# Attention rounds that prepare the first pair of head groups of the round after them, with half of the slot transfers begun from the scalar engine's own DMA queue

## What is computed

```python
x = window_attention(x)       # 16 heads of 16, window 64, rotary
x = gated_ffn(x)              # sigmoid(x Wr) * (relu(x Wk)^2 Wv), with a shift by one token
x = linear_attention(x)       # elu + 1 features, no softmax
h = layernorm(x); x = x + causal_attention(h) @ Wproj   # 16 heads, softmax over up to 1024 keys
x = x + moe(layernorm(x))     # 8 experts, top 2, capacity 1024
```

## Time and profile before

| | us |
|---|---|
| three runs, median (lowest, highest) | 2194.8 (2194.42, 2198.81) |
| the profiled execution | 2197.95 |
| its span in the trace | 2196.2 |

### The profile page before, as it was taken

How to read it: one execution, slowest core, us unless ns; L and a number is a source line. 1 busy time by engine, 2 the same in 40 slices (tenths; PEclk the granted TensorE clock), 3 DMA queues, 4 the chain that set the end, 5 groups by cost and what they waited for, 6 DMA issues and landing times. The chain is left out here.

```text
span 2196.2 us, 33587 instructions
## 1 busy us (share of the span) xinstructions
PE 1874.8 (85%) x11092; PEld 1115.5 (51%) x11092; DVE 1030.1 (47%) x2379; ACT 900.9 (41%) x1855; POOL 684.8 (31%) x991
## 2 busy tenths in 40 slices
PE   4998699899889989996998999699844999999990
PEld 2566345555443655554355555433332666666660
DVE  2456465487375547745744784576430000000014
ACT  1453255446527443662554465347511222222212
POOL 4203234213253320326232132532144233333220
PEclk8999799999979999997999999889956999999995
DMA  5600305520141543005044400423032233333215
GB/s 162 83 2 1 91 7 76 74 29 1 41 96 29 64 64 41 2 21 112 26 59 60 59 1 1 92 56 48 2 105 89 70 75 77 77 68 65 43 17 163
DMA packets 96381, 123.47 MB, mean 56 GB/s; under 512 B 15328, under 2 KB 69536, under 8 KB 96048
## 3 DMA queue, kind: packets, MB, share of 16 engines
q1 hardware_dynamic: 81360, 104.39, 23.8%
q0 software_dynamic: 14848, 16.85, 4.7%
HBM read 44.85 MB, written 25.58 MB: 32 GB/s over the span
## 5 line engine op out<-in xcount | busy, mean ns | idle before, releaser
L948 ACT ACTIVATE b_probs<-b_psum 128x512 f32<-128x512 f32 (+3 forms) x896 | 430.6, 538 | 266.2 <-PE b_psum L821 255.9
L1187 DVE TENSOR_REDUCE b_mneg<-b_psum 128x2 f32<-128x384 f32 (+5 forms) x608 | 337.8, 593 | 150.3 <-PE b_psum L805 144.8
L805 PE MATMUL b_psum<-b_qk 96*128 96x192 bf16 (+4 forms) x1280 | 325.9, 325 | 10.9 <-DVE b_mhalf L1187 5.6
L821 PE MATMUL b_psum<-b_qk 99*128 99x512 bf16 (+5 forms) x1344 | 295.0, 295 | 12.1 <-ACT b_probs L948 6.7
L836 PE MATMUL b_psum<-b_probs,b_v 128*32 128x512 f32 (+5 forms) x2688 | 234.3, 424 | 1.4 <-issue 1.3
L1552 DVE TENSOR_TENSOR b_ye<-b_psum,b_b2b 128x512 f32<-128x512 f32 x32 | 22.1, 692 | 429.1 <-PE b_psum L1507 423.6
L1507 PE MATMUL b_psum<-b_w,b_hid 128*128 128x256 f32 x1024 | 222.4, 379 | 0.8 <-ACT b_hid L1531 0.8
L1498 PE MATMUL b_psum<-b_xgt,b_w 128*128 128x512 f32 x512 | 222.2, 594 | 0.0
L1531 ACT ACTIVATE b_hid<-b_psum,b_b 128x512 f32<-128x512 f32 x128 | 88.0, 688 | 318.3 <-PE b_psum L1498 317.6
L1507 PEld LDWEIGHTS b_psum<-b_w,b_hid 128*128 128x128 f32 x1024 | 193.9, 190 | 27.6 <-ACT b_hid L1531 1.6
L821 PEld LDWEIGHTS b_psum<-b_qk 99*128 99x128 bf16 x1344 | 125.2, 100 | 145.4 <-ACT b_probs L948 72.7
(11 more groups left out here) (212 smaller groups left out, 2611.5 us busy)
## 6 DMA issues: line engine op xcount, KB each, us to landing
b_qk<-b_split SPq DMA_DIRECT2D x324, 128.0 KB, 5.8
b_w<-in_W SPq DMA_DIRECT2D x16, 1024.0 KB
b_qk<-b_split SPq DMA_DIRECT2D x120, 64.0 KB, 2.6
b_src<-in_x SPq DMA_DIRECT2D x4, 1024.0 KB, 5.7
before_last_norm<-b_early SPq DMA_DIRECT2D x4, 1024.0 KB, 4.5
b_o<-before_last_norm SPq DMA_DIRECT2D x4, 1024.0 KB
before_last_norm<-b_o SPq DMA_DIRECT2D x4, 1024.0 KB
normed<-b_y SPq DMA_DIRECT2D x4, 1024.0 KB, 4.5
```

What stands on the lines that cost most here:

```text
L805: ins = pe.matmul(out[:, i, :], q[0:KS, h, P * t:P * t + P], q[0:KS, HG + h, a:e], start=not last, stop=True, skip_group_check=True)
L821: ins = pe.matmul(out[:, i, :], q[0:KM, HG + h, P * t:P * t + P], q[0:KM, h, a:e], start=not windowed[g], stop=True, skip_group_check=True)
L948: act.activation(probs_of((g, h2, t))[:, heads[0]:heads[-1] + 1, a - BANK * h2:e - BANK * h2], bank, ACT.Exp, scale=SCALE).then_inc(s.exp_ ...
L1187: dve.tensor_reduce(out, in_bank(("max",) + x[1:], heads, e - a), AX.X, ALU.max, negate=True).then_inc(s.max_read, 1)
```

## The change

The rounds become: 4 near groups; then three rounds of 4 near and 4 far groups; then 4 far groups; then the route alone. The device loop is gone, the rounds are written out. Each of the three middle rounds also prepares the pair that the next round begins with (`coming`): a near pair of the next batch in the first two, for which `source`, `fetch` and `refill` are done again late in the round (behind `h_turn` and `out1`), and a far pair in the third. A round whose first pair is ready omits it and begins with its maxima. The second round isn't ready: it loads its own input (`own_x`) and prepares its pair 0 itself. Buffers of `qk` are given by a table. Group 8 takes the buffer of group 6, and group 9 that of group 4. At its end a round waits until the loads of the coming pair have landed. The 6 transfers of each group into the k half are a new kind, `send`, begun by ACT on its own queue. Group 0 is copied in halves only where the round isn't ready. Beside that `k1_exp` writes into `u.o` instead of a buffer of its own, and `v1_sum` comes after `k_feat`.

```diff
+QK_OF = {4: (0, 1, 2, 1, 0, 1), 8: (0, 1, 2, 0, 1, 2, 0, 2, 0, 1), 0: ()}
...
-    LANDING = {"load": 9.0, "spread": 2.2, "source": 3.0, "x3_in": 3.0, "x3_out": 3.0, "x4_out": 3.0, "z_out": 3.0}
+    LANDING = {"load": 7.0, "send": 7.0, "spread": 2.2, "source": 3.0, "x3_in": 3.0, "x3_out": 3.0, "x4_out": 3.0, "z_out": 3.0}
...
+        def fetch(late):
+            add(("source", late), "SP", 6.0, ("h_turn", 1, NC - 1) if late else None)
             for y in range(2):
                 for c in range(NC):
-                    add(("fetch", y, c), "PE", 0.45, ("source",))
-                    add(("refill", y, c), "ACT", 0.6, ("fetch", y, c))
+                    add(("fetch", late, y, c), "PE", 0.45, ("source", late), ("out1", 3) if late else None)
+                    add(("refill", late, y, c), "ACT", 0.6, ("fetch", late, y, c))
...
-            last = ("power",) + self.last_piece(g - RING, 1) if g >= RING else None
+            last = ("power",) + self.last_piece(self.behind(g), 1) if self.behind(g) is not None else None
...
-                        add(("load", g, a, slot, y), "SP", 0.46 if y is not None else 0.64, (kind, g // 2, q), last)
+                        add((("load", "send")[a], g, a, slot, y), ("SP", "ACT")[a], 0.46 if y is not None else 0.64, (kind, g // 2, q), last)
...
-        prep(0)
+        pairs = groups // 2 + (coming is not None)
+        if self.fetched:
+            fetch(0)
+        if not first:
+            prep(0)
         prep(1)
...
-            if n in (2, 4) and n + 2 < groups:
+            if n and n % 2 == 0 and n // 2 + 1 < pairs:
+                if n // 2 + 1 == groups // 2 and coming:
+                    fetch(1)
                 prep(n // 2 + 1)
...
+                if coming is not None:
+                    load_done(sp, groups + n)
...
+                elif kind == "send":
+                    send_slot(act, x)
...
-            attend(near, 0, later=later)
-            attend(far + near + far, 1)
-            with nc.Fori(1, B - 1) as b:
-                attend(far + near + far, b + 1, b - 1)
-            attend(far + far, None, B - 2)
-            attend((), None, B - 1)
+            attend(near, ahead=0, later=later)
+            for b in range(1, B):
+                more = b < B - 1
+                attend(near + far, ready=b > 1, ahead=b, own_x=rows_of(b) if b == 1 else None, coming=more,
+                       coming_x=rows_of(b + 1) if more else None, route=b - 2 if b > 1 else None)
+            attend(far, ready=True, route=B - 2)
+            attend((), route=B - 1)
```

More of the change, by code:

```diff
@@ L240, in place_of, with behind @@
     def place_of(self, g):
-        return self.of_kind[self.windowed[g]].index(g)
+        return self.of_kind[self.windowed[g]].index(g) if g < self.groups else g - self.groups
+    def behind(self, g):
+        return max((x for x in range(g) if self.qk_of[x] == self.qk_of[g]), default=None)
     def count_shared(self):
@@ L564, in load_done @@
     def load_done(eng, g, y=None):
-        if g:
-            eng.wait_ge(loaded[g], 16 * 2 * SLOTS)
-        else:
-            for n in range(2) if y is None else (y,):
-                eng.wait_ge(loaded[groups + n], 16 * 2 * SLOTS)
+        if g >= 2 or not ready:
+            if g:
+                eng.wait_ge(loaded[g], 16 * 2 * SLOTS)
+            else:
+                for n in range(2) if y is None else (y,):
+                    eng.wait_ge(loaded[2 * NG + 2 + n], 16 * 2 * SLOTS)
     def done(eng, *x):
@@ L617, in attend_and_pass_on, with send_slot @@
     sem = s._asdict()
+    def send_slot(eng, x):
+        _, g, a, slot, y = x
+        part = [slot in slots for slots in SLOTS_OF[a]].index(True)
+        eng.wait_ge((s.high_done, s.mid_done, s.low_done)[part], 4 * (g // 2 - plan.first) + (4 if y is None else 2 * y + 2))
+        if plan.behind(g) is not None:
+            eng.wait_ge(s.exp_done, order[("power",) + plan.last_piece(plan.behind(g), 1)] + 1)
+        cols = slice(0, T) if y is None else slice(BANK * y, BANK * y + BANK)
+        eng.dma_start(u.qk[plan.qk_of[g]][HD * slot:HD * slot + HD, HG * a:HG * a + HG, cols],
+                     u.split[HG * HD * (g % 2):HG * HD * (g % 2 + 1), a, part, cols]
+                     ).then_inc(loaded[g if g else 2 * NG + 2 + y], 16)
     xa = u.xa[:, :, 1:T + 1]
@@ L767, in _ @@
                     first = 2 * (plan.place_of(2 * g) // 2)
-                    if near and next_x is not None and t == 0 and not first:
-                        pe.wait_ge(s.fetched, 4)
+                    if t == 0 and 2 * g == groups and not near:
+                        done(pe, "h_take", 1, NC - 1)
+                    elif t == 0 and near and (2 * g == groups or own_x is not None):
+                        pe.wait_ge(s.fetched, 2 * NC * (1 + (2 * g == groups and own_x is not None)))
                     x_rows = u.xa[:, :, 1:T + 1] if near else u.xt
@@ L777, in _ @@
                 elif kind == "fetch":
-                    pe.wait_ge(s.src_in, 16)
-                    _, y, c = x
+                    _, late, y, c = x
+                    pe.wait_ge(s.src_in, 16 * (2 if late and own_x is not None else 1))
                     for t in range(4):
@@ L921, in _ @@
                         done(act, "k1_sum", k)
-                        if k >= 2:
-                            done(act, "k_feat", k - 2)
-                        act.wait_ge(s.added, NT * (groups // 2))
-                        ins = act.activation(u.kexp[k % 2], u.kfeat[:, half(k)], ACT.Exp, bias=u.minus[:, :])
+                        ins = act.activation(pair(u.o, k), u.kfeat[:, half(k)], ACT.Exp, bias=u.minus[:, :])
                     elif kind == "q_exp":
```

91 lines of the change are left out of this document (47 added, 44 removed).

## The result

The changed kernel takes 2297.4 us against 2196.8: ratio 1.046, 95% interval 1.042 to 1.050, so 100.6 us slower. I had said 2190, at most 2216.

The account below looks back on a forecast made before the run. PE, busy for 85% of 2196.2 us, was taken as the bound. Terms of 0 - 5 + 0 + 4 - 4 = -5 us against the profiled 2197.95 gave 2192.95; that execution lies 3.15 above the median, so 2190 us, range 2146 to 2216.

Parts of the forecast that it names:

- Boundaries, 0 each: At the three boundaries between rounds, PE's loss would be 32.1 us each against 32.0 before, so 0 each.
- my mark of 25 to 35: The prediction counts as wrong if the loss at a boundary between rounds leaves the span of 25 to 35 us.
- The rival that two queues overlap: At round ends, 24 transfers take 15 us on two queues; with other gains -44 us, 2151 in all; chance 0.25.
- PE's useful time stays, and only the lost time can change: At boundaries, work is moved, not removed: middle rounds still prepare four pairs each, so only PE's lost time can change.
- My own mark against me: The prediction counts as wrong if the stretches between boundaries lose over 10 us more or less.
- The first round, -5 (0 to -9): At the first round's start, two issuers begin the 64 KB transfers sooner: -5 us, bounds 0 and -9.
- The second round, 0 (-6 to +8): At the second round's start, waiting for its own input is paid back by shorter first maxima: 0, between -6 and +8.
- Maxima, -4 (-17 to +5): Inside rounds, maxima transfers have less ahead of them with half the slot transfers in the other ring: -4 us, -17 to +5.
- ACT's issues, +4 (0 to +35): In far stretches, issues moved to ACT stand between exponentials PE waits for, most of them hidden: +4 us, 0 to +35.
- Near stretches get worse: Rival: near groups come first and wait for their second pair's transfers, six more us in three rounds: 2207; chance 0.10.

Follow-up runs that it names:

- change_same_order_one_queue: The changed kernel with every compute engine's order kept and the scalar engine's 204 transfers merged into the sync engine's queue, against the kernel before: ratio 1.048.
- all_on_sync: The changed kernel with the k halves of a slot begun by the sync engine again, so one queue for all transfers, against the kernel before: ratio 1.036.
- before_landing_seven: The kernel before with only the planner's time from a slot's issue to its use lowered from 9 to 7 us: ratio 0.989, 2167.1 us.

## Why the prediction was wrong

**Boundaries, 0 each: right in size.** Predicted was 32.1 us each, measured is 93.2 / 3 = 31.1, though the third, at 35.4, lies just outside my mark of 25 to 35. By the finer count they won 4 us each. PE's idle time there was 18.5 to 21.1 us (said: about 20), the first exponentials came at 13.5 us (said: 12), and 24 transfers took about 25 us (bound 1.04 us each; I took 0.95). The rival that two queues overlap is out: 128 and 136 GB/s, where I had asked for 180. The rule in the Trainium skill, "DMA: Bandwidth & Descriptors", section "Issuing engines are not separate DMA queues", would have put the sum 7 us higher. Here the trace and change_same_order_one_queue agree with it: same order, one queue or two, 1.048 and 1.046. It has no price for a second issuer, though, and there is one: in the kernel before the same comparison is 1.018 and 1.031.

**The step that failed: "PE's useful time stays, and only the lost time can change", counted at the boundaries alone.** I took the bodies over at the loss they had in the kernel before, but for two small terms. My own mark against me was 10 us in the bodies. They lose 20 to 23 us more each. The boundaries did trade evenly. What changed is what had been taken as given, PE's waits inside the rounds, above all for transfers:

- **The buffer table** stood in the diff and in the words on the change, and the sum had no term for it. It costs 1.0 to 1.4%, 22 to 31 us. A slot transfer that becomes possible one group later is moved just when PE needs the maxima.
- **The first round, -5 (0 to -9): measured +24.** 15 of these are the table. Another 5 are the second round's input: PE waits 11.9 us behind the barrier where it waited 6.6. Its first exponentials came at 69.87, as in the earlier trace rows. The two queues didn't shorten the start; all_on_sync, with one, has them at 66.64. SP's own 18 issues at the start took from 38.23 to 55.21, 17 us for half of the 36 that had taken 24.92.
- **The second round, 0 (-6 to +8): measured about +44,** or about +32 without its new end, which belongs to the boundaries. A ready round saves a head, but the second isn't ready. It has a near head that waits for its input and its own slots: the head lost 36.1 us where 21.9 were lost, and its body 51.6 where 29.0 were. With the table and the urgency mended it is 406.6 us, against 367.5 in before_landing_seven. Of these 39 us, 13 are the moved pair and 12 the wait for b_mrow near its end. The remaining 14 aren't parted by any run. The head's wait, and the longest one of the body, in the changed kernel:

```profile
257.22 0.48 PE L814 MATMUL b_psum<-b_id,b_src 128*128 128x128 f32 x1 [11.93 <-DMA b_src<-in_x]
```
```profile
343.23 0.27 PE L851 MATMUL b_psum<-b_mask_k,b_id 128*128 128x128 bf16 x1 [8.19 <-DMA b_qk<-b_mrow]
```

- **Maxima, -4 (-17 to +5): measured +36.9** in PE's waits. What stands ahead of the maxima is set by when slots become possible and by the plan more than by how many queues there are: at the same order these waits are 81.4 us with one queue and 71.8 with two.
- **ACT's issues, +4 (0 to +35): +1.0%, 22 us,** inside the bounds, but partly by luck. The same order with all issues on SP is no faster. The 22 us are the order that the planner makes once ACT has 204 steps more; I costed an issue by its 0.64 us and never a new plan. The mechanism that I priced is there as well, 18 us more of PE's waiting for ACT at the same order, but two queues save at least as much in waiting for transfers.
- **LANDING** had no term either; it was worth -1%.

**Near stretches get worse**, with chance 0.10 and 6 us a round, was the rival that came nearest. It named the right wait (slots and maxima behind the second pair's transfers), but has a part of the loss only: near groups' waits for b_mrow in the three middle rounds are 41.7 us, where they were 30.5. PE's waits of 8.2 us at 343, 7.4 at 730, 6.8 at 815, 5.4 at 1135 and 7.2 at 1221 are all for near groups. The far groups, which had none before, have 22.6 us, among them 4.8 at 1359 and 7.4 at 1615. The range ended at 2216, since each rival was summed alone and none had the bodies, the first round and the second worse together.

How the 4.6% are made up, as far as the runs part it: the planner's number -1.1%; the table 1.0% (one queue); the late end of the round 2.4% by leaving the transfers out, of which 0.7% came back by planning them earlier, and 0.9% more with the maxima on ACT; ACT's queue 1.0% by the new order and nothing by itself. The remaining 1.3% or so is a balance that no run parted: the second round's head, which was only moved and not taken away, adds to it, and the shorter start of the ready rounds, which pays for their late ends, takes from it. Beside these the new place of the layer and the changes to `k1_exp` and `v1_sum` were never run alone. These parts are from different bases and needn't add up exactly.

## What to carry to other kernels

When a plan or a ring changes, price the bodies of the stages again: for each buffer ask when it comes free now and what small, urgent transfer then stands behind its refill, or lands beside it. Test a second queue with the order of all engines kept, since in a planned kernel an edit of one engine's steps reorders the others, and that can be the whole effect. Then compare what PE waits for, engine by engine: an even time can hide a gain and a loss of 20 us each. And a planner needs to be told what a step without followers is worth, and how long transfers take to land: the one number from 9 to 7 us won 1.1% in one line.

## What the runs showed of the hardware

- 12 KB alone in its own queue still took 9.4 us to arrive (609.70 to 619.15) while 24 transfers of 128 KB from another queue were moved. In the slots' own queue it took 10.7 behind 24 slots (610.52 to 621.17) and 7.5 behind 12 (122.92 to 130.46), from its issue on.
- Two queues moved slots at 128 and 136 GB/s, one at 121 to 130, at a DMA share of 1.06 or 1.07. From issue to landing a 128 KB slot took 7.5 (SP) and 7.8 us (ACT) with two queues, and 6.2 with one in all_on_sync (medians of the pages). The engines that begin transfers made no difference to the time at the same order (1.046 and 1.048), but in the other kernel the second queue cost 1.3%.
- Some 200 issues on ACT went with 18 and 27 us more of PE's waiting for ACT at the same order.
- Where PE had more pauses, its mean clock was lower: 0.94 or 0.95 in the bodies, where it was 0.96 or 0.97. From 1106 to 1462 PE was idle for 16.3 us more than from 1056 to 1378 before, and lost 23.1 us more. The later stretch is 34 us longer and holds 11 us more of useful work, so the difference of 7 us as the clock's part is an estimate.
